# Row tiles of layer 0's output in the last unit's step, low probabilities on two engines, scores ahead of maxima in the closing step

## The reference, cut to what matters

```
qn, kn, vn = layer_norm(x), layer_norm(ctx), layer_norm(ctx)     # over 512, gain ln1_g, shift ln1_b
Q, K, V = qn @ wq + bq, kn @ wk + bk, vn @ wv + bv               # 16 heads of 32
out = softmax(Q K^T / sqrt(32)) V                                # per batch and head, 100 x 722 scores
x1 = x + out @ wo + bo                                           # 800 rows x 512
y = layer_norm(x1, ln2_g, ln2_b)
x2 = x1 + gelu(y @ w1 + b1) @ w2 + b2                            # 512 -> 2048 -> 512
```

## Time and profile before

| what | us |
|---|---|
| median of 3 runs | 1488.65 (1487.69 to 1491.65) |
| the profiled execution, its own time | 1490.28 |
| its span in the profile | 1488.5 |
| TensorE busy (PE) | 1381.6, 93% of the span |
| VectorE busy (DVE) | 875.3, 59% |
| ScalarE busy (ACT) | 685.2, 46% |
| GpSimd busy (POOL) | 454.2, 31% |
| mean granted TensorE clock | 0.979 of full |

### The profile page before, as it was taken

One profiled execution on the slowest core, in us unless ns is written; L12 is line 12 of the kernel. 1 busy time (PEld: TensorE's weight loads), 2 busy tenths in 40 slices (PEclk: granted clock), 3 DMA queues, 4 the chain that ended last, 5 costly groups with the idle time before them and its releaser, 6 DMA issues.

```text
span 1488.5 us, 31512 instructions
## 1 busy us (share of the span) xinstructions
PE 1381.6 (93%) x12841; PEld 874.7 (59%) x12841; DVE 875.3 (59%) x1561; ACT 685.2 (46%) x1321; POOL 454.2 (31%) x504
## 2 busy tenths in 40 slices
PE   6987999999998659999999999999999999999997
PEld 4554666666665435545556666666666666666664
DVE  6766778778876657623434444555454455545565
ACT  3545667666755444411124444444444444444431
POOL 3124566666665652020001111121111121121223
PEclk9999999999999979999999999999999999999999
DMA  8227443343444006132442422224243222433421
GB/s 255 64 60 168 123 135 88 115 125 80 127 145 107 16 25 211 57 128 82 151 103 61 109 59 71 68 59 109 61 109 69 80 62 47 109 67 92 98 67 38
DMA packets 118109, 141.38 MB, mean 95 GB/s; under 512 B 49853, under 2 KB 92365, under 8 KB 115917
## 3 DMA queue, kind: packets, MB, share of 16 engines
q1 hardware_dynamic: 116777, 137.10, 33.9%
q10 hardware_dynamic: 1188, 2.27, 0.5%
HBM read 63.15 MB, written 22.17 MB: 57 GB/s over the span
## 4 chain that ended last, share of the span: by engine, by line
PE 46%; DVE 3%; issue 1%; ACT 1%; POOL 0%; POOLq 0%; ACTq 0%
PE attn_p_proj L1046 16%; PE attn_p_proj L1041 14%; PE attn_p_max L1066 3%; PE attn_p_sc L1248 2%; PE attn_p_sc L1097 2%; PE attn_p_sc L1096 2%; PE attn_p_pv L1125 1%; PE attn_p_proj L1186 1%; PE attn_p_pv L1124 1%; PE attn_p_pv L1126 1%; DVE attn_nmax L1612 1%; PE attn_p_max L1186 1%; ACT attn_probs L1394 1%; DVE attn_knat L1645 1%; ACT attn_knat L1423 0%
## 5 line engine op out<-in xcount | busy, mean ns | idle before, releaser
L1612 DVE TENSOR_REDUCE attn_nmax<-attn_p_max 100x1 f32<-100x722 f32 x256 | 231.8, 905 | 157.2 <-PE attn_p_max L1066 154.8
L771 POOL TENSOR_TENSOR attn_probs<-kernel_w_first,attn_probs 128x400 f16<-128x400 f32 x96 | 90.6, 944 | 674.5 <-ACT attn_probs L1394 674.5
L1046 PE MATMUL attn_p_proj<-kv_w_v,attn_ctxT 128*128 128x512 f16 (+1 forms) x1152 | 264.3, 379 | 0.0
L771 POOL TENSOR_TENSOR attn_probs<-attn_p,attn_probs 128x400 f16<-128x400 f32 x192 | 204.1, 1071 | 177.1 <-ACT attn_probs L1394 176.4
L1384 ACT ACTIVATE kernel_w_first<-attn_p_sc,attn_score_bias 128x400 f32<-128x400 f32 x192 | 113.7, 592 | 307.7 <-PE attn_p_sc L1097 307.7
L1041 PE MATMUL attn_p_proj<-attn_ctxT,kv_w_k 128*128 128x361 f16 x1536 | 249.1, 317 | 4.1 <-DVE attn_knat L1645 3.5
L1041 PEld LDWEIGHTS attn_p_proj<-attn_ctxT,kv_w_k 128*128 128x128 f16 x1536 | 144.5, 97 | 88.7 <-DVE attn_knat L1645 9.7
L1046 PEld LDWEIGHTS attn_p_proj<-kv_w_v,attn_ctxT 128*128 128x128 f16 (+1 forms) x1152 | 110.4, 101 | 111.0
L1384 ACT ACTIVATE attn_p<-attn_p_sc 128x400 f32<-128x400 f32 x192 | 96.5, 503 | 163.2 <-PE attn_p_sc L1093 156.3
L1046 PE MATMUL attn_p_proj<-l_w_v,attn_ctxT 128*128 128x512 f16 (+1 forms) x576 | 136.0, 387 | 10.3 <-DVE attn_vbuf L1651 10.2
L1041 PE MATMUL attn_p_proj<-attn_ctxT,kernel_w_first 128*128 128x361 f16 x768 | 131.1, 322 | 0.8 <-DVE attn_kscaled L1641 0.8
(11 more groups left out here) (244 smaller groups left out, 2573.2 us busy)
## 6 DMA issues: line engine op xcount, KB each, us to landing
kv_w<-attn_knat SPq DMA_DIRECT2D x128, 180.5 KB, 3.3
attn_kstack<-attn_knat SPq DMA_DIRECT2D x192, 90.2 KB, 2.2
ctx_turned<-attn_ctxT SPq DMA_DIRECT2D x8, 1444.0 KB, 8.1
attn_ctxT<-ctx_turned SPq DMA_DIRECT2D x8, 1444.0 KB, 8.5
attn_kstack_b<-attn_knat SPq DMA_DIRECT2D x64, 180.5 KB, 3.6
attn_c<-in_ctx_dram SPq DMA_DIRECT2D x35, 256.0 KB, 3.0
kv_w_v<-in_L_xattn_w_dram SPq DMA_DIRECT2D x7, 1024.0 KB, 5.6
q_parts<-attn_probs SPq DMA_DIRECT2D x16, 200.0 KB, 2.4
```

The costliest lines, as they stand in the source:

```text
L771: eng.tensor_tensor(probs[:r, g % 2, 1, t, :HG * SQ], p32[:r, t % 3, :], probs[:r, g % 2, 0, t, :HG * SQ], ALU.subtract).then_inc(p_lo_mad ...
L1046: last = pe.matmul(bank[:r, :], ctxT[:, cpar, ca, k, P * t:P * t + r], w_v[:, wa, k, c0:c0 + E], **flags)
L1612: dve.tensor_reduce(nmax[:SQ, hh:hh + 1], p_max[:SQ, :, :HALF], AX.XY, ALU.max, negate=True).then_inc(max_made, 1)
```

## The change

1. Row tiles 0 to 3 move into step 7: products in slots 3, 9, 15 and 21, sums two slots later, turns in slots 11, 17 and 23 of step 7 and 5 of step 8. Tile 4 has its product in slot 21 of step 8, its sum in slot 23 and its turn in slot 5 of step 9. They are counted in the alternation of `p_proj` with the projections (`use`, `row_use`).
2. `wo` is loaded by quarters and split in steps 5 and 6, the first part of `w1` by quarters in step 7 (slots 11 to 22). Buffers of x tiles, vectors and weights are placed anew, with the loads of SP's queue in another order; a store of tile 0 and its wait stand between the two stacks of keys in step 7.
3. In step 8 a slot's scores stand ahead of its maximum product on TensorE, and the maximum products of groups 1 to 3 alternate between `p_max` and `p_proj`.
4. In groups 2 and 3 of the last unit, the low probabilities of tiles 1, 3 and 5 are made by VectorE instead of GpSimd.
5. In step 9 VectorE normalises the last group; the last output is split, turned and copied in two parts (384 and 128 columns), in slots 12 and 14.
6. Context tiles 4 and 5 of batch 2 are loaded ahead of `queries_stored`, and no longer in unit 1.
7. In `mlp_up` two buffers of parts are placed further back in a room.

The diff, cut to its core:

```diff
         self.out_hi_t, self.out_lo_t, self.out_t = (10, 12, 14) if layer == 0 else (7, 8, 9)
         self.close = {i: divmod(i, 2) for i in range(10)} if layer == 1 else {}
-        self.next = [5, 6, 7, 8, 14, 15, 16, 17] if layer == 0 else [4, 5, 10, 11]
-        self.row_bias = [14, 16, 18, 20, 22]
-        self.row_base = [0, 6, 12, 18, 21]
-        self.row_acc, self.row_sum, self.row_pow, self.row_final, self.row_hi, self.row_lo, self.row_turn = 1, 4, 5, 7, 8, 11, 13
+        self.next = [4, 5, 10, 11]
+        last = (B if layer == 0 else 2 * B) - 1
+        self.next_hi = {(last - 2, 15): (0, 0), (last - 2, 16): (0, 1), (last - 1, 15): (0, 2), (last - 1, 16): (0, 3),
+                        (last, 11): (1, 0), (last, 13): (1, 1), (last, 17): (1, 2), (last, 21): (1, 3)}
+        self.next_lo = {(last - 2, 19): (0, 0), (last - 2, 20): (0, 1), (last - 1, 19): (0, 2), (last - 1, 20): (0, 3),
+                        (last, 12): (1, 0), (last, 14): (1, 1), (last, 18): (1, 2), (last, 22): (1, 3)}
+        self.row_bias = [3, 8, 13, 20]
+        self.row_base = [3, 9, 15, 21, 45]
+        self.row_place = [4, 9, 13, 17, 18]
+        self.row_acc, self.row_sum, self.row_pow, self.row_centre, self.row_final, self.row_hi, self.row_lo, self.row_turn = 0, 2, 3, 3, 4, 5, 7, 8
+        self.shared_lo = {(last, g, t) for g in (2, 3) for t in (1, 3, 5)} if layer == 0 else set()
         self.units = B if layer == 0 else 2 * B
         self.per = self.units // B
 
     def row_tile(self, s, j, ahead):
 
-        base = (s - self.units) * self.n + j - ahead
+        base = (s - self.units + 1) * self.n + j - ahead
         return self.row_base.index(base) if self.layer == 0 and base in self.row_base else None
 
     def misc(self, prep, proj, scores, outs):
 
         uses = []
+        layer0_end = self.layer == 0 and outs and not scores
         for j in range(self.n):
             g, t = divmod(j, KT)
             if prep and j in self.ctx:
                 uses.append(("ctx", self.ctx[j]))
+            if outs and j == self.out_t - 2 and layer0_end:
+                uses.append(("out", 0))
             if outs and j == self.out_t:
-                uses.append(("out", 0))
+                uses.append(("out", 1 if layer0_end else 0))
             if t == MAX_T and (scores if g < self.groups - 1 else proj):
                 uses.append(("max", g))
-            if outs and not proj:
-                T = self.row_tile(self.units if scores else self.units + 1, j, self.row_turn)
+            if outs and not prep:
+                T = self.row_tile(self.units - 1 if proj else self.units if scores else self.units + 1, j, self.row_turn)
                 if T is not None:
                     uses.append(("row", T))
         return uses
...
             return c32[:, n % NCB, :], c_loaded[n % NCB], 16 * (n // NCB + 1)
 
+        def use(u, a):
+
+            rows_ahead = sum(place <= a + i for i, place in enumerate(sl.row_place)) if layer == 0 and u == U - 1 else 0
+            return NPROJ * u + a + rows_ahead
+
+        def closing_max(u, g):
+            return layer == 0 and u == U - 1 and g > 0
+
+        def max_banks(u, g, hh):
+            return p_proj if closing_max(u, g) and hh % 2 else p_max
+
+        def row_use(T):
+            return NPROJ * (U - 1) + sl.row_place[T]
+
+        def next_stage(i, k):
+            return c32[:, NCB - 2 + k] if i == 1 and k < 2 else kscaled[:, k % 2, :E]
+
...
                 def unit(u, prep):
-                    load_q(u, u % 2, u)
                     if u == U - 1:
                         sp.wait_ge(proj_ready, NPROJ * u)
                         sp.wait_ge(ctxT_moved[0], 16 * (B // 2))
-                        load_next_weight(0)
+                        load_mid(0)
                         sp.wait_ge(proj_freed, NPROJ * (u - 1) + 8)
                         sp.dma_start(bo_row, mid_vectors[0].partition_broadcast(P)).then_inc(bo_loaded, 16)
+                        sp.dma_start(g2_row, mid_vectors[1].partition_broadcast(P)).then_inc(g2_loaded, 16)
+                    load_q(u, u % 2, u)
+                    if u == U - 1:
+                        sp.dma_start(b2_row, mid_vectors[2].partition_broadcast(P)).then_inc(b2_loaded, 16)
+                        load_mid(1)
                         sp.wait_ge(c_lo_made, KT * B)
                         sp.wait_ge(stats_made, KT * B)
-                        load_next_weight(1)
-                    if prep:
+                        load_next_tile(1, 0)
+                        load_next_tile(1, 1)
+                        load_mid(2)
+                    if prep and u > 1:
                         load_ctx_tile(u + 1, 4)
                         load_ctx_tile(u + 1, 5)
                     stack_k(u, u % 2, 0)
+                    if u == U - 1:
+                        store_mid(0)
+                        sp.wait_ge(mid_stored[0], 16)
+                        sp.wait_ge(mid_centred, 1)
+                        load_mid(3)
+                        sp.wait_ge(k_lo_made, ET * U)
+                        load_next_tile(1, 2)
+                        load_next_tile(1, 3)
+                    if u in (U - 3, U - 2):
+                        sp.wait_ge(k_lo_made, ET * (u + 1))
+                        load_next_tile(0, 2 * (u - U + 3))
+                        load_next_tile(0, 2 * (u - U + 3) + 1)
                     stack_k(u, u % 2, 1)
                     if u + 2 < U:
...
                     store_queries(m)
+                for t in range(NCB, KT):
+                    load_ctx_tile(2, t)
                 queries_stored()
                 place_onehot([1])
             else:
...
                     sp.wait_ge(ctxT_moved[i], 16 * (B // 2))
-                sp.wait_ge(next_lo_made, ET)
-                for T in range(EARLY):
-                    sp.dma_start(mid[T], x_d[ROW0[T]:ROW0[T] + P, :]).then_inc(mid_loaded[T], 16)
-                sp.wait_ge(next_lo_made, 2 * ET)
-                for dst, vector, sem in zip((g2_row, b2_row), mid_vectors[1:], (g2_loaded, b2_loaded)):
-                    sp.dma_start(dst, vector.partition_broadcast(P)).then_inc(sem, 16)
+                store_mid(1)
+                sp.wait_ge(mid_stored[1], 16)
+                sp.wait_ge(mid_centred, 2)
+                load_mid(4)
+                for T in range(2, EARLY - 1):
+                    store_mid(T)
                 sp.dma_start(b1_col[:], b1_d.rearrange("(k p) -> p k", p=P), allow_slow_non_contiguous=True).then_inc(b1_loaded, 16)
-                for T in range(EARLY):
-                    sp.wait_ge(mid_summed, T + 1)
-                    sp.dma_start(x1_d[ROW0[T]:ROW0[T] + P, :], mid[T]).then_inc(mid_stored, 16)
+                store_mid(EARLY - 1)
                 sp.wait_ge(b1_loaded, 16)
-                sp.wait_ge(mid_stored, 16 * EARLY)
+                for T in range(1, EARLY):
+                    sp.wait_ge(mid_stored[T], 16)
             else:
...
+                    pe.wait_ge(proj_freed, row_use(EARLY - 2) + 1)
                 kr = MR if layer == 0 else P
                 for n in range(2):
-                    last = pe.matmul(p_max[:SQ, n, :HALF], qstack[0][:kr, par, h, :],
+                    last = pe.matmul(max_banks(u, g, hh)[:SQ, n, :HALF], qstack[0][:kr, par, h, :],
                                      kstack[0][:kr, par, h, n * HALF:(n + 1) * HALF], start=True, stop=True)
                 last.then_inc(max_ready, 1)
 
...
                     g, t = divmod(j, KT)
+                    scores_first = layer == 0 and s == U
+                    if scores_first:
+                        scores(s, s - 1, 1 - par, g, t)
                     if g < NG - 1 and has_scores and t < HG:
                         max_scores(s - 1, 1 - par, g + 1, t)
                     if g == NG - 1 and proj and t < HG:
                         max_scores(s, par, 0, t)
-                    if has_scores:
+                    if has_scores and not scores_first:
                         scores(s, s - 1, 1 - par, g, t)
                     if layer == 1:
                         turns(s, kind, j)
...
                 dve.reciprocal(orecip[:SQ, g % 2, :], pv_sb[:SQ, g % 2, :, DK]).then_inc(recip_made, 1)
 
+            def shared_prob_lo(u, g, t):
+
+                if (g, t) == (2, 1):
+                    dve.wait_ge(p_lo_made[1], lo_count(u, g - 1, KT - 1))
+                prob_lo(dve, u, g, t)
+
+            def last_normalise():
+
+                cols = slice(E - P, E)
+                recip = orecip[:SQ, 1, :].rearrange("p (h o) -> p h o", o=1).to_broadcast([SQ, HG, DK])
+                dve.wait_ge(o_made, U * NG - 1)
+                dve.wait_ge(recip_made, U * NG)
+                dve.tensor_tensor(osum[:SQ], pv_sb[:SQ, 1, :, :DK], pv_sb[:SQ, 1, :, DK + 1:], ALU.add).then_inc(o_summed, 1)
+                dve.wait_ge(o_summed, U * NG)
+                dve.tensor_tensor(osum[:SQ], osum[:SQ], recip, ALU.mult).then_inc(o_normed, 1)
```

(30 more changed lines are left out.)

149 lines of the change are left out of this document (94 added, 55 removed).

## The result

The changed kernel takes **1469.8 us** (median of 4 runs, 1467.3 to 1472.6); the kernel before, run beside it, 1490.15 (4 runs, 1487.7 to 1492.6). The ratio is 0.9864 with a 95% interval of 0.9838 to 0.989: faster. The forecast was 1459.6, its range 1451 to 1472. The side was right and the time 10.2 us above the forecast: the gain of the medians is 20.4 instead of 29.1 us, and the kernel before was 1.5 us slower in these runs than in the ones that the sum started from.

The account below looks back on a forecast made before the run. Ordinary layer 0 steps were read as TensorE-bound, steps 1 and 7 to 9 as held by waits. Terms -8.4 + 0 + 6.2 - 18.5 - 8.4 = -29.1 took 1490.3 to 1461.2, median 1459.6 us; range 1451 to 1472.

Parts of the forecast that it names:

- (a): Step 1: loading context tiles 4 and 5 of batch 2 early removes ScalarE's 9.9 us wait; gain 8.4 us.
- what is late next: Step 1: stacking unit 1's keys, wanted by slot 18, becomes the next late transfer; charged 1.0 us (0 to 4).
- rival 1: Step 1's stall moves to the key DMAs and slot 18 waits; gain only 2 to 3, 1465.5 us; chance 0.10.
- (b): Steps 5 and 6: splitting w_o's four tiles there is covered by TensorE; cost 0 (0 to 3 us).
- (c): Step 7: takes four row products and three turns, loses late loads and half the weight splits; cost 6.2 us (3 to 10).
- rival 5: Step 7: GpSimd waits for x and bias, work behind stops and the clock falls; slower, 1493 us; chance 0.03.
- (d): Step 8: four products fewer, second maxima bank, six low probabilities on VectorE; 34.0 us long, gain 18.5 us.
- (e): Step 9: only tile 4's end remains beside the last group's values; 8.4 us long, gain 8.4 us.
- Groups 2 and 3 run at its pace and ScalarE's: Step 8: GpSimd and ScalarE set the length of groups 2 and 3; 14.5 us.
- Rival 2: Step 8: low probabilities on VectorE exclude GpSimd's through the shared port; 5.7 us more, 1465.3 us; chance 0.12.
- Rival 3: Step 8: TensorE's clock stays at 1.2 GHz, the step takes 42 instead of 34; 1467.6 us; chance 0.10.
- Rival 4: Step 8: row tiles weren't what held it, the maxima's chain keeps it near 46; 1471.6 us; chance 0.07.

Follow-up runs that it names:

- e1: Changed kernel with context tiles 4 and 5 of batch 2 loaded where the kernel before loads them, behind unit 1's query load: 1474.04 us.
- e2: Changed kernel with unit 1's first twelve key-stacking DMAs ahead of the one-hot row DMAs and the context store on SP: 1466.80 us.
- e8: Changed kernel with every row tile's turn one slot later: 1467.01 us.
- e4: Changed kernel without the sharing, all low probabilities of the closing step made by GpSimd: 1470.84 us.
- e3: Changed kernel with the last probabilities' low part made ahead of tile 4's bias, sum and statistics on VectorE: 1470.51 us.
- e9: Changed kernel with tile 4's chain based four slots earlier and the last low part ahead of other work on VectorE: 1469.79 us.
- e7: Changed kernel with every score matmul of the closing step issued three times in a row: 1470.20 us.
- e6: Changed kernel with the maximum product ahead of the scores in each closing-step slot, second bank kept: 1468.76 us.
- e12: Changed kernel with the output's low part in the closing step made by VectorE instead of GpSimd: 1467.41 us.
- e5: Changed kernel with a single bank for the closing step's maxima: 1475.09 us.
- b1: Changed kernel with the edits of e2, e3, e8, e9 and e12 together: 1464.3 us, ratio 0.9846 to the kernel before.

## Why the prediction was right in sign and too large in size

**(a) Step 1, gain 8.4 forecast: 4.7 and 6.2 measured** in two profiles. What it removes was right: e1 shows the 8.8 us wait for the transfer when the loads are late again. The term that failed is "what is late next", charged at 1.0 with bounds of 0 to 4: step 1 would be 52.1 without it (e2) and is 56.4 or 57.9, so it costs 4.3 to 5.8, past the upper bound. (The removal itself was worth 10.5 where the working has 9.4.) The working had the transfers right: it let the stacking DMAs be issued from 130 and the twelfth land at about 144, and they were issued from 130.5 and it landed at 143.3. What it had wrong is when they are wanted. It moved slot 18 up to about 143; TensorE stood there at 138.0 (140.2 in the second profile). The next step shows what to expect: its slot 18 comes 38.0 us after its start (159.6 to 197.6), which from 101.8 is 139.8. Nor did it ask what stood between the query stores and the stacking and could go: four one-hot DMAs and a store, and a query load, 125.5 to 130.5. This is **rival 1's mechanism**, with a gain twice as large as it gave.

**(b) Steps 5 and 6, 0 forecast: 1.0 measured**, 0.5 in each (52.5 to 53.0), inside its bounds. Some of the weight tiles' operations aren't covered; which, no run shows.

**(c) Step 7, cost 6.2 forecast: 8.1 measured**, inside 3 to 10. Clock 1.00 and products of 2.75 us came as said, GpSimd doesn't wait for x (so rival 5 is out). The working charged VectorE's delay at 1.5 us, all of it at the maxima. TensorE waited 2.1 us for maxima and 4.2 at the three turns for VectorE's low part, which it had put at nothing. e8, which moves the turns, shortens step 7 by 3.1, and steps 7 to 9 without tile 4's product by less than 1.

**(d) and (e) Steps 8 and 9, from 69.3 to 42.4 forecast: 48.1 to 49.6 measured**, a gain of 20 to 21 instead of 26.9. This is the largest miss. Groups 0 and 1 took 9.1 and 6.1 us where 9.9 and 5.7 were forecast. Groups 2 and 3 were given 14.5, 2 for tile 4's product and 1.9 for the clock, 18.4 in all; they took 10.4 and 13.2 up to the last values, 23.6. (These are counted at the score products, which run up to two tiles ahead. Counted at the exponentials, which start at 490.30, 499.19, 507.33 and 515.88 and end at 524.00, the four groups took 8.9, 8.1, 8.6 and 8.1 us, so group 2 isn't a slow one.) The step that failed is "Groups 2 and 3 run at its pace and ScalarE's", GpSimd's being meant. e4 speaks against it: with GpSimd busy 92% instead of 74% of the stretch up to tile 4's product, the stretch is as long. So does the profile, in which ScalarE is busy 9.7 of these 14.2 us. I had added busy times where the length comes from handovers: scores, exponential, low part, and back to TensorE, crossed by maxima, splits and turns. The second part is the end: tile 4's product, then its bias, sum and statistics on VectorE, ahead of the last low part. TensorE stands 4.92 us there; e3 and e9 show that this can't be had back by VectorE's order alone, and e4 that 1.2 us of it can by leaving the low parts to GpSimd. The clock was charged at 1.9 for gaps; at tile 4's product alone it costs 0.6 to 2.2. What sets the 8 to 9 us of a group is open: neither GpSimd's load (e4), nor TensorE's busy time (e7), nor the order of scores and maxima (e6), nor the output's low part (e12) is it alone. Step 8 took 38.7 (40.2, 39.5 and 40.3 in the other unaltered profiles), at the edge of its bounds of 30 to 39; step 9 was 9.4 (8.4 forecast, inside 7.5 to 10.5).

**The rivals.** Rival 2: the lock can be seen on single operations (below) and on GpSimd's low parts beside tile 3 in group 0, but not on the shared low parts, where GpSimd's take 0.94 to 0.96 us up to tile 4's product with and without sharing. Undoing the sharing gives 1.2 us, and at the end of the step, by order and not by the lock. Rival 3: its condition came true, the clock in step 8 is 0.72 and lower than before, and its price was 8 us where the product that is on the path shows 0.6 to 2.2. It took all of TensorE's work for what step 8 waits on. Rival 4: step 8 at 39 to 40, not 46, and the waits for maxima down to 0.6. In e5 the bank's share is 2.9 us or a little more. That the row work is the rest is argued by elimination and not shown; moving the row tiles back was not tried.

The account of the miss, against the first profile: 3.7 in (a), 1.0 in (b), 1.9 in (c), 5.6 in (d) and (e), less the 3.6 outside these steps, is 8.6 (29.1 less 20.5); all four parts erred on the costly side. The result lies outside the forecast's own 1452 to 1468. It lies in the range only because that was stretched to rival 4's 1472, and rival 4's mechanism did not hold, so the range held by luck. Of the signs named for being wrong, two came: the wait for stacked keys at slot 18, and step 8 over 40 in two of four profiles. Step 1 isn't near 53. The first MLP matmuls took 9.76 us where 10.67 was expected.

## What to carry to other kernels

When a late transfer is moved forward in a queue, look up who was next behind it and what stands before that one: an order on SP has to be sorted by when each transfer is needed, the whole stretch at once. In the closing step here no engine was busy over 75%, and its length couldn't be read from busy times: taking six operations off its second-busiest engine, GpSimd, brought nothing and cost 1.2 us at the end, while a second buffer in the loop brought 3 us of the 4 us of waits that it removed. When two chains end together, shortening one brings nothing (e3, e9); five edits together gave 2 us there where single ones gave at most 1. And before comparing two profiles of such a stage, take out what the clock did to the one long product on the path: it hid e4's 1.2 us and made half of b1's 3.9.

## What the runs showed of the hardware that I had not expected

The same wait varies from run to run, and only in part by the transfer: at slot 18 of step 1 it was 5.33 and 2.98 us in two profiles of one program, and 1.89 to 3.02 in eight others with the same step 1 (e3 to e9 and e12). In the two profiles of the changed kernel it ended at 143.35 and 143.13; what differs is when TensorE got there, 138.0 and 140.2. So of the 2.4 us by which the wait differs only 1.5 show in step 1 (57.9 and 56.4), and the wait can't be read as the cost.

Filling TensorE with repeated matmuls cost no time here and lifted its clock: 193 more recorded matmuls, 0.5 us more busy time, clock 0.72 to 0.98 (e7). It paid only at the one product that is on the path.

VectorE's two-input operations do stretch beside GpSimd's. Tile 4's bias addition takes 1.30 us when it starts at 524.68 inside a low probability on GpSimd that began at 524.49; in e3, where it starts behind that one, the same addition takes 0.68:

```profile
524.49 0.94 POOL L799 TENSOR_TENSOR attn_probs<-attn_p,attn_probs 128x400 f16<-128x400 f32 x1 [2.92 <-ACT attn_probs L1460]
```

```profile
524.68 1.30 DVE L1786 TENSOR_TENSOR attn_ctxT<-attn_ctxT,attn_rrow 128x512 f32<-128x512 f32 x1
```

```profile
526.51 0.68 DVE L1786 TENSOR_TENSOR attn_ctxT<-attn_ctxT,attn_rrow 128x512 f32<-128x512 f32 x1
```

From 524.68 to the end of GpSimd's operation at 525.43 are 0.75 us, and the addition is 0.62 longer. In the kernel before, the five final scalings of the earlier trace rows, 1007 ns in the mean, took 0.74, 0.74, 1.43, 1.37 and 0.75 us: the mean is of two kinds. The Trainium skill ("SBUF — State Buffer", "SBUF: two separate sides") calls the shared port pair an exclusive lock between such operations. By it the addition would take 0.68 + 0.75 = 1.43 us; the measured 1.30 agrees but for 0.13.
